# Interleaving the three small operations of the reciprocal norms with the softmax's maximum and subtraction on VectorE

## The reference

```python
def attn_layer(x, Wqkv, qs, ksc, Wo):          # x: token-shifted
    q, k, v = split(x @ Wqkv)                   # 16 heads of 64
    q = rotary(l2norm(q) * qs); k = rotary_inv(l2norm(k) * ksc)
    sim = einsum(q, k_two_windows) * 8          # windows of 32, each sees 64 keys
    attn = softmax(where(mask, -big, sim))
    return (attn @ v_two_windows) @ Wo
def ffn_layer(x, ...):
    xn = layernorm(x) * g + b
    a, gate = split(xn @ W1 + b1)
    return a * gelu(gate) @ W2 + b2
for i in range(6):
    x = attn_layer(shift(x), ...) + x
    x = ffn_layer(shift(x), ...) + x
```

## Time and profile before

| | us |
|---|---|
| median of 3 runs | 1732.7 |
| lowest and highest run | 1731.18, 1740.07 |
| span of the profiled execution, first to last instruction | 1731.0 |
| VectorE busy | 1446.3 (84%) |
| ScalarE busy | 1425.6 (82%) |
| GpSimd busy | 1311.9 (76%) |
| TensorE busy (matmul) | 1639.0 (95%) |
| mean granted TensorE clock | 0.986 |

### The profile page before, as it was taken

How to read it: one execution, slowest core, us unless ns; L and a number is a source line. 1 busy time by engine, 2 the same in 40 slices (tenths; PEclk the granted TensorE clock), 3 DMA queues, 4 the chain that set the end, 5 groups by cost and what they waited for, 6 DMA issues and landing times.

```text
span 1731.0 us, 68758 instructions
## 1 busy us (share of the span) xinstructions
PE 1639.0 (95%) x25970; PEld 1277.2 (74%) x25970; DVE 1446.3 (84%) x3011; ACT 1425.6 (82%) x2851; POOL 1311.9 (76%) x1305
## 2 busy tenths in 40 slices
PE   7779999999999999999999999999999999999995
PEld 5657777777777777777777777777777777777773
DVE  4499888888888888888888888888888888888884
ACT  3367888888888888888888888888888888888885
POOL 6088877877877787787778778787877877777765
PEclk9799999999999999999999999999999999999997
DMA  4111111111111111111111111111111101111000
GB/s 140 41 38 43 35 33 36 30 48 38 41 32 30 36 36 42 49 30 32 30 36 42 49 36 30 32 30 48 38 41 36 30 27 38 35 30 32 28 24 26
DMA packets 41426, 66.40 MB, mean 38 GB/s; under 512 B 7072, under 2 KB 16032, under 8 KB 41376
## 3 DMA queue, kind: packets, MB, share of 16 engines
q1 hardware_dynamic: 40224, 65.38, 12.7%
q10 hardware_dynamic: 1152, 0.34, 0.1%
HBM read 20.61 MB, written 1.05 MB: 13 GB/s over the span
## 4 chain that ended last, share of the span: by engine, by line
PE 61%; ACT 28%; issue 6%; DVE 4%; ACTq 1%; DMA 0%; POOL 0%; DVEq 0%; POOLq 0%
PE ps_qs L530 12%; PE ps_po L530 9%; PE ps_q L530 8%; PE ps_a L530 7%; PE ps_tk L530 7%; PE ps_f L530 6%; PE ps_po L650 5%; ACT p_bd L943 4%; PE ps_k L530 4%; PE ps_v L530 4%; ACT squares L949 4%; ACT L1053 3%; ACT L1050 3%; ACT q_t L943 3%; ACT prob L987 2%
## 5 line engine op out<-in xcount | busy, mean ns | idle before, releaser
L427 POOL TENSOR_TENSOR qk<-qk,rnorm 128x512 f32<-128x512 f32 x384 | 393.6, 1046 | 176.6 <-DVE rnorm L1284 176.1
L419 POOL TENSOR_TENSOR qk<-qk,qk_rot 128x512 f32<-128x512 f32 x384 | 483.8, 1282 | 0.0
L434 POOL TENSOR_TENSOR prob<-prob,row_inv 128x512 f32<-128x512 f32 x192 | 200.7, 1045 | 92.8 <-DVE row_inv L1301 92.8
L1289 DVE TENSOR_REDUCE row_max<-ps_qs 128x8 f32<-128x512 f32 x191 | 132.0, 691 | 164.8 <-PE ps_qs L530 164.8
L943 ACT COPY p_bd<-ps_po 64x512 f32<-64x512 f32 x378 | 219.1, 580 | 58.8 <-PE ps_po L650 56.4
L1264 DVE TENSOR_REDUCE ssq<-squares 128x8 f32<-128x512 f32 x384 | 261.4, 681 | 3.4 <-ACT squares L949 3.4
L530 PEld LDWEIGHTS ps_qs<-k_t,q_t 64*32 64x32 f32 x12224 | 179.2, 107 | 69.0 <-issue 68.9
L943 ACT COPY attn_t<-ps_po 128x512 f32<-128x512 f32 x191 | 112.5, 589 | 133.2 <-PE ps_po L530 133.1
L530 PE MATMUL ps_qs<-k_t,q_t 64*32 64x64 f32 x12224 | 210.1, 218 | 0.0
L530 PE MATMUL ps_po<-p_bd,v_back 128*64 128x64 f32 x3056 | 193.2, 225 | 0.0
L530 PEld LDWEIGHTS ps_po<-p_bd,v_back 128*64 128x64 f32 x3056 | 163.1, 137 | 35.8 <-issue 17.0
(11 more groups left out here) (237 smaller groups left out, 4082.7 us busy)
## 6 DMA issues: line engine op xcount, KB each, us to landing
v_back<-v_own SPq DMA_DIRECT2D x192, 192.0 KB, 2.4
w_raw<-in_wqkv SPq DMA_DIRECT2D x48, 192.0 KB, 2.4
v_back<-v_own SPq DMA_DIRECT2D x96, 64.0 KB, 2.1
wo_sb<-in_wo SPq DMA_DIRECT2D x12, 256.0 KB, 2.9
w_sb<-in_w SPq DMA_DIRECT2D x6, 341.0 KB, 3.1
w_sb<-in_w SPq DMA_DIRECT2D x6, 192.0 KB, 2.7
x_in<-in_x SPq DMA_DIRECT2D x4, 256.0 KB, 4.2
out<-s_out SPq DMA_DIRECT2D x8, 128.0 KB, 1.9
```

What stands on the lines that cost most here:

```text
L419: nc.gpsimd.tensor_tensor(qk[:, s, i, :], qk[:, s, i, :], qk_rot[:, s, i, :], ALU.add).then_inc(added, 1)
L427: nc.gpsimd.tensor_tensor(heads(qk[:, s, i, :]), heads(qk[:, s, i, :]), rnorm[:, s, 8 * i:8 * i + 8].unsqueeze(2).to_broadcast([P, 8, HEAD ...
L434: nc.gpsimd.tensor_tensor(heads(prob[:, s, :]), heads(prob[:, s, :]), row_inv[:, s, :].unsqueeze(2).to_broadcast([P, 8, HEAD]), ALU.mult). ...
L1289: V.tensor_reduce(row_max[:, s, :], heads(ps[:]), AX, ALU.max).then_inc(max_done, 1)
```

## The change

`newton` and `softmax_shift` are cut into their single operations. The loop's body issues them in the order rn_a (unit u-1), maximum (u-3), rn_b (u-1), subtraction (u-3), rnorm (u-1). Every wait stays with its operation. The drain calls the two functions as before.

```diff
-            def newton(c, s, used):
+            def newton_product(c, s):
                 dve.wait_ge(rn_started, c + 1)
                 V.scalar_tensor_tensor(out=rn_a[:, s, :], ...).then_inc(rn_step, 1)
+
+            def newton_square(c, s):
                 dve.wait_ge(rn_step, 2 * c + 1)
                 V.tensor_tensor(rn_b[:, s, :], rn_a[:, s, :], rn_0[:, s, :], ALU.mult).then_inc(rn_step, 1)
+
+            def newton_finish(c, s, used):
                 dve.wait_ge(rn_step, 2 * c + 2)
                 wait(dve, k_normed, used)
                 V.scalar_tensor_tensor(out=rnorm[:, s, :], ...).then_inc(rnorm_done, 1)
-            def softmax_shift(u, s, ps=ps_qs):
+            def row_maximum(u, s, ps=ps_qs):
                 dve.wait_ge(s_done, u + 1)
                 V.tensor_reduce(row_max[:, s, :], heads(ps[:]), AX, ALU.max).then_inc(max_done, 1)
+
+            def subtract_maximum(u, s, ps=ps_qs):
                 dve.wait_ge(max_done, u + 1)
                 wait(dve, pt_done, u - 1)
                 V.tensor_tensor(heads(prob[:, s, :]), ...).then_inc(sub_done, 1)
...
+                    if live(u - 1):
+                        newton_product(u - 1, (j - 1) % 2)
                     if live(u - 3):
-                        softmax_shift(u - 3, (j - 3) % 2)
+                        row_maximum(u - 3, (j - 3) % 2)
                     if live(u - 1):
-                        newton(u - 1, (j - 1) % 2, u - 2)
+                        newton_square(u - 1, (j - 1) % 2)
+                    if live(u - 3):
+                        subtract_maximum(u - 3, (j - 3) % 2)
+                    if live(u - 1):
+                        newton_finish(u - 1, (j - 1) % 2, u - 2)
                     sum_squares(u, 0, j % 2)
                     rotate(n, j, 0)
```

More of the change, by code:

```diff
@@ L1285, in newton @@
                                        op0=ALU.add, op1=ALU.mult).then_inc(rnorm_done, 1)
-            def softmax_shift(u, s, ps=ps_qs):
+            def newton(c, s, used):
+                newton_product(c, s)
+                newton_square(c, s)
+                newton_finish(c, s, used)
+            def row_maximum(u, s, ps=ps_qs):
                 dve.wait_ge(s_done, u + 1)
                 V.tensor_reduce(row_max[:, s, :], heads(ps[:]), AX, ALU.max).then_inc(max_done, 1)
+            def subtract_maximum(u, s, ps=ps_qs):
                 dve.wait_ge(max_done, u + 1)
@@ L1294, in softmax_shift @@
                                 ALU.subtract).then_inc(sub_done, 1)
+            def softmax_shift(u, s, ps=ps_qs):
+                row_maximum(u, s, ps)
+                subtract_maximum(u, s, ps)
             def sums(u, s):
```

## The result

The changed kernel takes 1815.9 us (median of 4 runs, 1814.4 to 1819.9), against 1732.3 us of the kernel before measured beside it: ratio 1.047, 95% interval 1.044 to 1.050. The profiled execution has a span of 1813.7 us, 82.7 more than before.

A forecast was written before the change was run, and what follows sets the result against it. Bound: ScalarE's stretch, then TensorE's, in each 33.63 us round. 36 rounds x 1.34, 8 x 0.99 make 56, plus 5 at the start: +61 on the median 1732.7, 1794 us; range 1762 to 1817.

The forecast's parts named there:

- the two stretches: Round of 33.63 us: ScalarE without a gap from 834.19 to 847.00, then TensorE without idle time to 867.82.
- j = 1, +0.60: First small operation carries ScalarE's late root start to maximum and subtraction: +0.60 us on ScalarE's stretch, bounds 0.55 and 0.80.
- VectorE's shorter tail: From the subtraction to the next sum of squares, 0.71 instead of 1.12: rnorm and GpSimd 0.41 us earlier, no time saved itself.
- j = 2, +0.25: First operation beats GpSimd's weight rounding by 0.07; the square is held instead, TensorE +0.25 us (0.15 to 0.30).
- GpSimd first: Rival, chance 0.22: in j = 2 the weight rounding precedes the first operation; 1.92 us per round, 1815 us.
- j = 3, +0.49: GpSimd's additions, following VectorE's reciprocal of j = 2, hold the first operation: TensorE +0.49 us (0.3 to 0.6).
- j = 0, 0: First operation held by GpSimd's additions, at most 0.15 us against ScalarE's two copies; taken as 0.
- The last 8 rounds: Rounds without weight rounding: j = 2 in time, j = 3 +0.39, with j = 1 0.99 us in all (0.85 to 1.2).
- The start: Batches 0 to 3: first operation held by GpSimd delays some ten units; 5 us taken, bounds 0 and 12.
- Wait only: Rival, chance 0.15: first operation not held by GpSimd, only its wait on ScalarE counts; 0.71 per round, 1764 us.
- Faster: Rival, chance 0.03: earlier rnorm ends TensorE's wait on GpSimd's normalising sooner, 0.41 us per round, 1715 us.
- No change: Rival, chance 0.04: ScalarE takes up the +0.60 in a gap not seen in the chain; 1733 us.

The follow-up runs named there:

- only_j1: New order in j = 1 only, the kernel before's order in j = 0, 2 and 3: 1766.3 us, ratio 1.020.
- keys_first: Kernel before, but in j = 1 ScalarE squares the keys of u behind the copies of the turned queries and keys: 1711.0 us, ratio 0.9865.
- one-input runs: Small operations as one-input reductions, Newton step left out: changed order 1763.3 us; new order except in j = 1 1738.1 us; order of before 1730.7 us.
- one_after: Changed kernel's order and waits, each small operation a one-element reduction with one SBUF input, Newton step left out: 1763.3 us, ratio 1.016.

## Why the prediction was right, and where it fell short

**What bounds the round** was read rightly: the two stretches, the 0.87 in front of the feed-forward product and the rest as TensorE's own. `only_j1` and `keys_first` show it from both sides.

**j = 1, +0.60.** Measured 0.77. The ScalarE part is right (0.57). The 0.20 of GpSimd's hold was my upper bound and not my value, on the ground that GpSimd's chain gets 0.41 earlier by VectorE's shorter tail. This is the step that failed. The tail did not get shorter in j = 0: from the subtraction to the end of the reciprocal it is 3.87 after (839.68 to 843.55) and 3.88 before, and GpSimd's product was still running when the first operation came. What I missed is a wait in `rotate` (line 1250): the rotary product of the queries may overwrite qk only when TensorE has turned the queries of u-2. Turn and rotary product of j = 0, before and after:

```profile
835.40 0.60 PE L530 MATMUL ps_qs<-ident,qk 128*128 128x128 f32 x4
836.22 0.69 DVE L1256 TENSOR_TENSOR qk<-ps_q,table 128x512 f32<-128x512 f32 x1
```

```profile
840.61 0.60 PE L530 MATMUL ps_qs<-ident,qk 128*128 128x128 f32 x4
841.43 0.69 DVE L1256 TENSOR_TENSOR qk<-ps_q,table 128x512 f32<-128x512 f32 x1 [0.38 <-PE ps_qs L530]
```

In j = 0 the turn doesn't wait for the subtraction. It follows TensorE's own products, 0.01 after ScalarE's exponential in both kernels (835.39, 840.60), and the rotary product follows it by 0.82 in both. So all that the shorter tail gained became idle time. In j = 1, 2 and 3 the turn waits for the very subtraction that stands in front (1.42, 0.17 and 0.42), which shows in j = 1 as VectorE's idle 0.19. As long as three small operations stood between, they filled that time.

I also took ScalarE's path to the feed-forward product for the longer one (0.60 against TensorE's 0.54). By the trace the two meet. The product starts 0.20 after the copy of the turned keys ends in both kernels (846.80 to 847.00 and 852.78 to 852.98), but now TensorE's own product in front of it ends at 852.98 too, and the 0.87 of idle time is used up.

**j = 2, +0.25.** Measured 0.33. VectorE came first, as forecast, and the square paid. The margin was 0.33 instead of 0.07, since GpSimd came later than I thought, by the same step: the rounding starts 7.98 after the subtraction of j = 1 (849.84 to 857.82), where I had 7.73. So the square was held longer. The rival "GpSimd first" is refuted although its number, 1815, is nearly the measured one. That is luck: its terms were 0.80 in j = 2 and 0.52 in j = 3, measured are 0.33 and 0.64.

**j = 3, +0.49.** Measured 0.64. The mechanism is right: additions hang on the reciprocal of j = 2, and the first operation on them. The tail from the subtraction to the end of the reciprocal is 3.54 in j = 2 (858.79 to 862.33) against 3.83 before, -0.29 instead of -0.41.

**j = 0, 0.** Right: part 4 grows by 0.06 only. I had not priced these 0.06: a turn that starts after a wait takes 0.66 instead of 0.60.

**The last 8 rounds**, 0.99: measured 1.42, by the same terms (0.77 in j = 1, 0.58 in j = 3, 0.06 behind it). **The start**, 5: measured 6.7; what it is made of was not taken apart. **Sum.** (0.17 + 0.08 + 0.15 + 0.06) = 0.46 short per round, 36 times, is 17 us, 0.43 x 8 = 3 us, 2 us at the start: the 22 us between 1794 and 1816. The 0.77 of j = 1 and the start lie inside my bounds; 0.33, 0.64 and 1.42 lie above 0.30, 0.60 and 1.2. By the bounds alone the range ended at 1815; the time is inside because I had widened the range to its neighbours.

"Wait only" is refuted by the one-input runs: its 1764 is the 1763.3 us of `one_after`, where the three are not held, and the changed kernel is 53 us above that. The hold is a rule of the Trainium skill (SBUF — State Buffer, "Who interferes with whom"): two SBUF inputs on VectorE against a GpSimd instruction that reads SBUF; a reduction is not affected. The runs agree with both halves, 0.37 to 0.80 for the held operations with two inputs in the new order's rows above and 0.16 to 0.17 for the reductions with one. The held clamps are a third case, with one input and no reduction. "Faster" and "No change" had nothing for them: in j = 1 rnorm came later (850.45, 9.85 after the exponential of j = 0, against 8.76 before), and in the loop TensorE never waited for GpSimd's normalising.

## What to carry to other kernels

A small operation in front of a critical one brings along everything it can wait for: its semaphore, here 0.57 us per round behind a table load, and GpSimd's hold, here 1.12 us. Before moving a small VectorE operation, look in the trace whether it is sometimes held (the three here, and the clamp too), and lay its new place over GpSimd's timeline. Price the moved operations' old place too: the three of them had filled the time in which the rotary product waits for TensorE. If an engine's stretch bounds a loop, look first for an operation in it whose reader has slack; one such move gave 1.3% where the interleaving cost 4.7%.

## What the runs showed that I had not expected

The hold can last over many GpSimd operations. In the profile of `one_after`, in the part ahead of the loop that all kernels share, VectorE's timeline has

```profile
16.12 4.38 DVE L1158 SCALAR_TENSOR_TENSOR rn_a<-ssq_c,rn 128x16 f32<-128x16 f32 x1 [0.53 <-ACT rn L890]
```

beside GpSimd's

```profile
15.87 0.86 POOL L388 TENSOR_TENSOR table<-qk,prob 128x128 f32<-128x128 f32 x2
...
19.97 0.50 POOL L404 CAST w_hi<-w_raw 128x384 fp32r<-128x384 f32 x1
20.66 0.99 POOL L407 TENSOR_TENSOR w_lo<-w_raw,w_hi 128x384 fp32r<-128x384 f32 x1 [0.18 <-POOL w_hi L404]
```

GpSimd works from 15.87 to 20.47 without a gap, in ten table products and a cast, and the small operation got through only in the gap of 0.18, at 20.50. So here the hold outlasted the running GpSimd operation many times over, which the prediction's rule (held until the running one is over) doesn't cover. In the kernel before the same operation took 0.17 at the same place (it started at 15.76), and the two small ones behind it took 0.35 and 0.38 beside the same table products. In the loop held operations ended behind a single GpSimd operation, also where the next followed at once. What decides between the two stays open; it was not tried.
